# First attention of a one-layer model: value pieces moved from even steps to odd steps

## Reference

```python
h = 0.15 * level_emb[levels(token_ids)]
x = layernorm(h)
Q, K, V = heads(x @ Wq.T + bq), heads(x @ Wk.T + bk), heads(x @ Wv.T + bv)
scores = (Q K^T + BD) / sqrt(16)     # BD[i, j] = Q[i] . Er[255 - i + j]
attn = softmax(scores)
h = h + (attn V) @ Wo.T + bo
...
```

## Time and profile before

| what | value |
|---|---|
| median of 3 runs | 792.87 us (789.66 to 793.83) |
| profiled execution, its own time | 789.15 us |
| its span, first to last instruction | 787.3 us |
| PE busy | 739.9 us, 94% |
| DVE, ACT, POOL busy | 58%, 47%, 25% |
| mean granted TensorE clock | 0.995 |
| level attention, first build to last sum | about 45 to 226 us of the span |

### The profile page before, as it was taken

How to read it: one execution, slowest core, us unless ns; L and a number is a source line. 1 busy time by engine, 2 the same in 40 slices (tenths; PEclk the granted TensorE clock), 3 DMA queues, 4 the chain that set the end, 5 groups by cost and what they waited for, 6 DMA issues and landing times. The chain is left out here.

```text
span 787.3 us, 19021 instructions
## 1 busy us (share of the span) xinstructions
PE 739.9 (94%) x7221; PEld 561.6 (71%) x7222; DVE 459.9 (58%) x1105; ACT 367.1 (47%) x608; POOL 195.1 (25%) x300
## 2 busy tenths in 40 slices
PE   3899999999999998999997989999999999999994
PEld 1377777777767886455554864555899999999993
DVE  7777777777636564999982865512334444443441
ACT  4677777767634444366764212201233333333330
POOL 5410000000003433333230540265132222323232
PEclk9999999999999999999999999999999999999997
DMA  4400000000011345444464900022432323233231
GB/s 165 175 2 2 2 3 2 2 2 2 3 48 41 104 138 159 130 122 123 126 244 138 366 26 16 29 87 79 157 50 44 54 43 51 47 47 49 45 48 20
DMA packets 70545, 58.97 MB, mean 75 GB/s; under 512 B 7552, under 2 KB 62152, under 8 KB 70480
## 3 DMA queue, kind: packets, MB, share of 16 engines
q1 hardware_dynamic: 62048, 47.61, 19.7%
q0 software_dynamic: 7152, 9.38, 7.3%
q10 hardware_dynamic: 1280, 1.08, 0.4%
HBM read 35.02 MB, written 22.95 MB: 74 GB/s over the span
## 5 line engine op out<-in xcount | busy, mean ns | idle before, releaser
L1488 POOL DMA_INDIRECT out<-ex_Y,ex_to x39 | 60.6, 1554 | 166.1 <-DVE ex_Y L1763 163.1
L652 ACT ACTIVATE la_PT<-ps 128x512 f32<-128x512 f32 x128 | 69.5, 594 | 46.5 <-PE ps L553 46.1
L1214 DVE TENSOR_REDUCE fa_m<-ps 128x2 bf16<-128x512 f32 x128 | 84.2, 683 | 6.7 <-PE ps L1083 5.5
L1717 DVE TENSOR_TENSOR ex_hT<-ps,ex_sl 128x512 f32<-128x512 f32 x39 | 27.0, 692 | 98.9 <-PE ps L1554 98.9
L1184 ACT ACTIVATE fa_PT<-ps 128x1024 f32<-128x1024 f32 x64 | 65.5, 1024 | 39.5 <-PE ps L1098 39.4
L1561 PE MATMUL ps<-WD,ex_hT 128*128 x312 | 74.0, 380 | 1.6 <-DVE ex_Y L1763 0.9
L1554 PEld LDWEIGHTS ps<-ex_xT,V 128*128 128x128 f32 x640 | 74.5, 192 | 1.1 <-ACT ex_xT L1607 0.2
L1554 PE MATMUL ps<-ex_xT,V 128*128 128x128 f32 x640 | 74.8, 275 | 0.0
L1554 PEld LDWEIGHTS ps<-ex_xT,XS 128*128 128x128 f32 x608 | 70.8, 192 | 0.9
L1554 PE MATMUL ps<-ex_xT,XS 128*128 128x128 f32 x608 | 71.0, 275 | 0.0
L671 DVE TENSOR_TENSOR la_SM<-ps,la_SA 128x512 bf16<-128x512 f32 x64 | 44.3, 692 | 37.7 <-ACT la_SA L634 19.1
(11 more groups left out here) (262 smaller groups left out, 1442.1 us busy)
## 6 DMA issues: line engine op xcount, KB each, us to landing
QK<-qk_parts SPq DMA_DIRECT2D x192, 64.0 KB, 2.3
qk_parts<-pj_parts SPq DMA_DIRECT2D x16, 384.0 KB, 2.8
expert_in<-zfill SPq DMA_DIRECT2D x1, 5070.0 KB, 16.1
ex_XR<-expert_in SPq DMA_DIRECT2D x39, 130.0 KB, 2.1
WG<-in_e_gate SPq DMA_DIRECT2D x8, 512.0 KB, 6.9
WU<-in_e_up SPq DMA_DIRECT2D x8, 512.0 KB, 10.5
WD<-in_e_down SPq DMA_DIRECT2D x8, 512.0 KB, 10.0
out<-HS SPq DMA_DIRECT2D x4, 512.0 KB, 4.9
```

What stands on the lines that cost most here:

```text
L652: nc.scalar.activation(PT[:, n // 2 % 2, jh, n % 2], ps[:, 2 * (n % 2) + jh], ACT.Exp, scale=QK_SCALE).then_inc(s_exp[jh], 1)
L1214: nc.vector.reduce_max(m[:, b % 2, grp, 2 * k:2 * k + 2], ps[:, h % 2].rearrange("p (f j) -> p f j", f=2), AX.X).then_inc(s_max, 1)
L1488: nc.gpsimd.indirect_dma_start(out=outs, out_offset=bass.IndirectOffsetOnAxis(ap=to[:, n:n + 1], axis=0), in_=Y[:, n], in_offset=None, com ...
```

## The change

Seven of the eight pieces of a run go to odd steps, at offsets 1, 3, 5, ... 13, and stand behind `sum_levels`, ahead of `subtract_max`. The first piece of a run (offset 0, an even step) stays in the gap. Before, the offsets were 0, 2, 4, ... 12 and 13. ScalarE's and VectorE's code is not changed; `keep_out` follows `piece_of`, and so comes in the odd steps, ahead of that step's `exp`, as before.

```diff
-    AT = [2 * x for x in range(PIECES - 1)] + [2 * PIECES - 3]
+    AT = [0] + [2 * x - 1 for x in range(1, PIECES)]
...
                     turn(n)
                     if n + 1 < N:
                         build(n + 1, 0)
-                    if piece_of(n):
+                    if piece_of(n) and n % 2 == 0:
                         weigh(*piece_of(n), min(n + FIRST, UNITS))
                     if n + 1 < N:
                         build(n + 1, 1)
                     if n % 2 and n >= 3:
                         for jh in range(2):
                             sum_levels((n - 3) // 2, jh)
+                        if piece_of(n):
+                            weigh(*piece_of(n), min(n + FIRST, UNITS))
                     subtract_max(n)
                     if n + FIRST < UNITS:
                         make_unit(n + FIRST)
```

## The result

The changed kernel takes 797.19 us (median of 15 runs, 794.65 to 802.21) where the kernel before takes 792.15 (15 runs, 788.87 to 795.12): ratio 1.0072, 95% interval 1.0054 to 1.0089. The ratio makes it slower by 5.7 us; the two medians are 5.0 us apart.

A forecast was written before the change was run, and what follows sets the result against it. The prediction took odd steps as bound by PE and even steps without a piece by ACT and DVE. Its terms, 10.26 + 1.08 - 5.98 - 0.22 = +5.1 us on the median of 792.87, gave 798.0 us, range 793.0 to 801.5.

The forecast's parts named there:

- The bound: Level attention: even steps bound by ACT and DVE unless a piece is in them, odd steps by PE.
- The price behind the sums: Odd steps, between sums and subtraction: each of 18 moved pieces adds 0.57 us, together +10.26 us.
- Its division: Split of a piece's 0.57 us behind the sums: 0.47 multiplication, 0.10 for leaving the 32x32 tiles.
- What the even steps give back: Even steps losing pieces: 16 give back 0.32 us each, steps 60 and 62 give 0.43 each, together -5.98 us.
- Steps 31 and 47: Pieces already in odd steps go from gap to behind the sums: 0.57 in place of 0.68 us, together -0.22 us.
- The new wait: Unit's load waits for ACT's piece copy: PE stands 0.16 us, 0.10 hidden, 0.06 seen, 18 times, +1.08 us.
- the piece fits under the sums' tail: Rival, odd steps: loads and some matmuls run during the sums' last 0.41 us; sum -3.1, 789.8 us; chance 0.05.
- a free switch between the two: Rival: no cost between sums and pieces, piece 0.47 us; sum +3.1 or +2.1, 795.0 to 796.0 us; chance 0.14.
- The third rival: Bank wait seen in full: `keep_out` holds ACT, `exp` 0.08 late, PE's 0.16 stall unhidden; +6.9, 799.8 us; chance 0.17.

The follow-up runs named there:

- odd_gap: Kernel before with the changed offsets (odd steps), each piece left in the gap between the halves of a build; ratio 1.0068 against the kernel before.
- behind_sums_bank7: Changed kernel with the piece's result in PSUM bank 7 in place of 6; ratio 1.0071 against the kernel before.
- ahead_of_sums: Changed kernel with odd-step pieces between the build's second half and the sums; level attention 186.77 us, +4.04 against the kernel before, no timed ratio.
- before_twice: Kernel before with each piece's eight matmuls issued twice, in the gap; level attention 192.78 us, +10.05 against the kernel before, no timed ratio.
- piece_twice: Changed kernel with each piece's eight matmuls issued twice in a row; level attention 198.59 us, +15.86 against the kernel before, no timed ratio.
- even_late_bank6: Kernel before with pieces moved behind the build's second half, result still in bank 6; level attention 184.55 us, +1.82 against the kernel before.
- even_late_bank7: Kernel before with pieces moved behind the build's second half and the result in bank 7; ratio 0.9999 against the kernel before.

## Why the prediction was right

**The bound.** Right. Even steps without a piece are bound by the chain over ACT and DVE, 3.34 us from subtraction to odd turn in odd_gap, behind_sums_bank7 and ahead_of_sums alike, and odd steps by PE; odd_gap shows that moving the pieces between them costs 6.2 us with nothing else changed, and before_twice that the slack of an even step ends with one piece.

**The price behind the sums, +0.57 (18 pieces, +10.26 us).** Right to the hundredth, with the sums' end at 1.00. Its division was off: 0.43 for the multiplication and 0.14 beside it, by piece_twice. The prediction divided the 0.35 us between the first and the fourth round by three, and the first round is longer than the others (0.13 against 0.11). The Trainium skill (TensorEngine Tiling (Array Packing), Key Properties) says that changing the tiling mode drains the engine. The runs agree with it so far: a piece pays on both sides, 0.68 us between full-width groups, and shares one side's price if the sums are there, 0.57. That the cost is a drain was not shown, only that 0.09 is paid on entering and 0.11 on leaving, and neither by a second copy.

**What the even steps give back, 0.32 and 0.43 (-5.98 us).** Right: without the bank wait the even step is 2.45 us (odd_gap, bank 7), and steps 60 and 62 went from 3.19 and 3.18 to 2.75.

**Steps 31 and 47 (-0.22).** Right without the bank wait: 3.81 in the gap, 3.71 behind the sums in bank 7.

**The new wait (+1.08 us).** Right in its place and too small. The copy of the piece ended 0.52 behind the subtraction as worked out (93.82 + 0.38 = 94.20), but the unit's load came 0.11 after it and not 0.05, so PE stood 0.22 us and not 0.16. The slack hid 0.11 of it, `la_SA` starting 0.04 behind the build's end (95.23 + 0.40 = 95.63, 95.67). So 0.10 to 0.11 was seen for each of 18, not 0.06, some 0.8 us in all where 0.7 was missing: the term of the sum that was mis-sized. It accounts for the stage's +5.82 where +5.1 was forecast.

**The rivals.** That the piece fits under the sums' tail is refuted by its 0.57, and so is a free switch between the two, which would have left little more than the 0.43 of the multiplication. The third rival had `exp` late behind `keep_out`: `exp` started at 0.44, as before, since ACT took it 0.30 us after a copy that lasts 0.38. The full bank wait of that rival exists only where no slack follows, as in even_late_bank6.

What stays open: why the load in bank 6 comes 0.11 us behind the end of the copy, while in bank 7 it comes 0.05 behind. By the code, in bank 6 a wait for the unit copy, long satisfied, stands ahead of the late one, and in bank 7 none does. The builds of even_late_bank7 show the same two sizes, 0.11 with waits ahead of the late one and 0.05 without. That the waits ahead cause it is likely and not shown: no run removed them alone.

## What to carry to other kernels

When steps of two kinds alternate, find out for each kind which engine's chain ends last before moving work between them: the same 0.68 us of TensorE work cost 0.32 in a step that waits for others and all of it in a step that does not. A tidier order inside the step (next to work of a like kind) was worth 0.10. And when a result's buffer is shared with the next work on the engine, check the distance between writing it and needing the buffer again: moving the writer closer to the end of the step made a wait that had been hidden.

## What the runs showed of the hardware

- Eight float32 matmuls on 32x32 tiles with 128 moving columns, on four column groups, take 0.43 us, and 0.14 more once per group, of which 0.11 lies between its last round and the next group, whether that has full width or 128x32 tiles. Behind full-width matmuls another 0.09 is paid on entering, and behind the sums none.
- A ScalarE copy of 128x256 has a record of 0.38 us, but the next instruction started 0.30 us behind its start (93.82 and 94.12). A record's length is not the time for which it keeps the next one back.
- After a late semaphore TensorE's next weight load started 0.05 us behind the end of the releasing record in some places and 0.11 in others (0.11 in bank 6 and 0.05 in bank 7 behind the piece's copy; 0.11 and 0.05 behind `exp` in steps 19 and 21 of even_late_bank7). The 0.11 came where other waits, long satisfied, stood ahead of the late one.
